# TensorE's column-half groups put next to each other, x and the ranks in other PSUM banks, and three moves on ScalarE and VectorE, in an attention + routed FFN kernel

## What is computed

```python
qkv = x @ W_attn + b_attn                       # [2, 2048, 768], 16 heads of 16
scores = einsum('bhtd,bhsd->bhts', q, k) / 4    # causal and j >= i - 64, per head
out = softmax(scores) @ v
x = layernorm(x + out @ W_proj + b_proj)
expert_idx = argmax(softmax(x @ Wr.T))          # one expert per token
inter = sum_e mask_e * gelu(x @ W1[e] + b1[e])
y = inter @ Wo + bo + x
out = layernorm(layernorm-with-gamma-beta(y) + x)
```

## Time and profile before

| what | us |
|---|---|
| median of 3 runs | 527.08 (524.29 to 529.04) |
| the profiled execution, its time | 529.32 |
| the profiled execution, its span in the trace | 527.6 |
| TensorE busy, share of the span | 486.1, 92% |
| VectorE busy | 427.4, 81% |
| ScalarE busy | 355.8, 67% |

### The profile page before, as it was taken

The page is one execution under the profiler, slowest core; times in us unless marked ns, Lnnn a source line. Parts: engine busy times, 40 slices in busy tenths (PEclk is TensorE's granted clock), DMA queues, the critical chain, the costliest instruction groups (busy, mean ns, idle before and its releaser), DMA issues. The chain is left out here.

```text
span 527.6 us, 24512 instructions
## 1 busy us (share of the span) xinstructions
PE 486.1 (92%) x8574; PEld 429.5 (81%) x8574; DVE 427.4 (81%) x1122; ACT 355.8 (67%) x796; POOL 321.6 (61%) x563
## 2 busy tenths in 40 slices
PE   7899999999999999899968797999999999999980
PEld 6778888888888888788857686888999999999970
DVE  5658888778977898778887567999999989999882
ACT  6576868677776877586857564666666766766850
POOL 8712545454464546354546447777888878888773
PEclk9999999999999999999999899999999999999996
DMA  7785768886778697686772122222345654532100
GB/s 200 194 240 174 205 206 235 209 206 186 231 207 220 183 253 193 193 229 191 187 197 58 42 63 62 73 62 64 83 117 187 199 175 162 171 130 79 44 23 8
DMA packets 90184, 80.96 MB, mean 153 GB/s; under 512 B 36502, under 2 KB 83871, under 8 KB 90018
## 3 DMA queue, kind: packets, MB, share of 16 engines
q1 hardware_dynamic: 86720, 70.95, 48.5%
q0 software_dynamic: 3248, 8.41, 4.7%
q10 hardware_dynamic: 98, 0.04, 0.0%
HBM read 43.50 MB, written 23.55 MB: 127 GB/s over the span
## 5 line engine op out<-in xcount | busy, mean ns | idle before, releaser
L1407 PE MATMUL ps<-v_even,w_hi 128*128 128x128 f16 x1024 | 141.2, 219 | 0.9 <-issue 0.8
L1389 PE MATMUL ps<-wo_hi,ks 128*128 128x256 f16 (+1 forms) x576 | 128.5, 273 | 7.3 <-DVE ks L1090 6.4
L833 ACT ACTIVATE probs<-ps,b1T 128x128 f32<-128x128 f32 (+1 forms) x312 | 85.5, 360 | 67.4 <-PE ps L1407 65.6
L1407 PE MATMUL ps<-v_even,w_lo 128*128 128x128 f16 x512 | 108.2, 219 | 0.1
L1407 PEld LDWEIGHTS ps<-v_even,w_hi 128*128 x1024 | 96.8, 98 | 3.9 <-issue 1.6
L1161 DVE TENSOR_REDUCE mx<-ps 128x4 bf16<-128x512 f32 x128 | 82.8, 684 | 10.2 <-PE ps L1458 9.7
L743 POOL CAST att_hi<-att 128x256 f16<-128x256 f32 x32 | 12.6, 394 | 114.7 <-DVE att L1218 114.7
L1389 PE MATMUL ps<-wo_lo,ks 128*128 128x256 f16 (+1 forms) x288 | 78.5, 273 | 0.0
L1090 DVE TENSOR_TENSOR ks<-probs,ks 128x512 f16<-128x512 f32 (+1 forms) x72 | 69.2, 961 | 9.0 <-ACT ks L840 5.5
L1507 PE MATMUL ps<-v_odd,probs 128*64 128x17 f32 x1024 | 69.7, 210 | 2.5 <-issue 2.5
L852 ACT ACTIVATE probs<-ps 128x512 f32<-128x512 f32 x128 | 69.5, 611 | 3.1 <-PE ps L1484 2.1
(11 more groups left out here) (246 smaller groups left out, 1279.2 us busy)
## 6 DMA issues: line engine op xcount, KB each, us to landing
qk_s<-qk_room SPq DMA_DIRECT2D x32, 256.0 KB, 3.0
w_in<-in_L_ffn_W_dram SPq DMA_DIRECT2D x16, 512.0 KB, 5.8
v_odd<-slots SPq DMA_DIRECT2D x64, 128.0 KB
qs<-qk_s SPq DMA_DIRECT2D x16, 384.0 KB
ks<-qk_s SPq DMA_DIRECT2D x16, 384.0 KB, 5.6
ks<-qk_s SPq DMA_DIRECT2D x32, 144.0 KB
v_even<-v_odd SPq DMA_DIRECT2D x63, 68.0 KB, 3.6
qk_s<-qk_room SPq DMA_DIRECT2D x32, 128.0 KB, 2.6
```

The costliest lines, as they stand in the source:

```text
L833: last = nc.scalar.activation(g[1 - p][:, ic, n * w:(n + 1) * w], ps_h[1 - p][:, half, col + n * w:col + (n + 1) * w], ACT.Gelu, bias=b1T[ ...
L1389: ins = mm(ps_y[p][0:m], h[p][hs][:, ic, 0:m], wo[ws][:, ic, :], start=n == 0, stop=n == 3 * IC - 1)
L1407: up_ins = mm(ps_h[1 - p][:, half, col + m * w:col + (m + 1) * w], weights(ws, m, k, ic), sT[1 - p][ss][:, k, at], start=k + n == 0, stop= ...
```

## The change

TensorE: in all iterations but 0, `scores(0)` and `scores(1)` move behind the projection and the transposes of x, so that the half groups follow each other. x's transposes write bank 4 and wait for `exps(0)` of the iteration before. The ranks write bank 6 (the last pair bank 1), no longer wait for `v_out` and `lx_done`, and `values(0)` waits for `place_done` in place of the projection. `mx` is 128 columns wide, so its transposes are full groups. ScalarE: v's copy goes between `maxima_rows(0)` and `maxima_rows(1)`. VectorE: `y` and `logits` go ahead of `maxima(0)`; the w1 split goes ahead of the copy `attT`. Both engines: two halves of w1 in each even iteration and none in an odd one, in place of one in each.

```diff
-        mx = [sb(f"mx{k}", [P, P - ALIGNED], bf16) for k in range(2)]
+        mx = [sb(f"mx{k}", [P, P], bf16) for k in range(2)]
...
         def ps_x(t):
-            return ps[:, 0 if t >= LEAD else 4 + t % 2, 0:CC * P].rearrange("p (k t) -> p k t", k=CC)
+            return ps[:, 4 if t >= LEAD else 4 + t % 2, 0:CC * P].rearrange("p (k t) -> p k t", k=CC)
...
-        ps_rank = ps[:, 1, 320:320 + 3 * E].rearrange("p (a e) -> p a e", a=3)
+        def ps_rank(pair):
+            return ps[:, 6 if pair < TILES // 2 - 1 else 1, 320:320 + 3 * E].rearrange("p (a e) -> p a e", a=3)
...
-        ps_mx = ps[0:P - ALIGNED, 2, 0:P].bitcast(bf16).rearrange("p (e m n) -> p e m n", e=2, m=CC)
+        ps_mx = ps[:, 2, 0:P].bitcast(bf16).rearrange("p (e m n) -> p e m n", e=2, m=CC)
...
         def w1_halves(it):
-            halves_at = range(it - 1, it) if it < TILES - 3 else range(2 * it - TILES + 2, 2 * it - TILES + 4)
+            halves_at = range(it - 2, it if it % 2 == 0 else it - 2) if it < TILES - 3 else range(2 * it - TILES + 2, 2 * it - TILES + 4)
...
# ScalarE
+                cur = a_tile(it)
+                if cur:
+                    act.wait_ge(mxT_done, it + 1)
+                    maxima_rows(0)
                 if a_tile(it + 1):
...
                         v_odd[m % VRING][:, :, 0:HD], ps_v[:, 0:C].rearrange("p (h d) -> p h d", d=HD), ACT.Copy)\
                         .then_inc(v_out, 1)
-                cur = a_tile(it)
                 if cur:
-                    act.wait_ge(mxT_done, it + 1)
-                    maxima_rows(0)
                     maxima_rows(1)
...
# VectorE
-                maxima(0)
-                maxima(1)
-                for t in turned(it) if it > FIRST else ():
-                    x_low(t)
                 if a_tile(old):
...
+                maxima(0)
+                maxima(1)
+                for t in turned(it) if it > FIRST else ():
+                    x_low(t)
...
+                for n in w1_halves(it):
+                    split_w1(n)
...
                     nc.vector.tensor_copy(attT[:, :, :, :], ps_attT).then_inc(attT_out, 1)
-                for n in w1_halves(it):
-                    split_w1(n)
...
# TensorE
                         wait(pe, att_done, done)
+                        wait(pe, place_done, (done - 1) // 2)
...
-                scores(0)
+                    scores(0)
+                    scores(1)
                 if a_tile(old):
...
-                    wait(pe, place_done, old // 2)
...
-                scores(1)
                 for t in turned(it):
...
                     if t >= LEAD:
-                        pe.wait_ge(qkh_done, t)
-                        pe.wait_ge(qkl_done, t)
+                        wait(pe, exp_done, 4 * (it - 1) + 1)
...
+                if it != 0:
+                    scores(0)
+                    scores(1)
                 values(0)
...
                     pe.wait_ge(onehot_done, old // 2 + 1)
-                    pe.wait_ge(v_out, upto(it + 1))
-                    pe.wait_ge(lx_done, upto(it + 1))
```

More of the change, by code:

```diff
@@ L858, in maxima_rows @@
                     nc.scalar.activation(q.rearrange("p (i h) n -> p i h n", i=STRIPS),
-                                         ps_mx.rearrange("p e m n -> p (e m) n").unsqueeze(1)
+                                         ps_mx[0:P - ALIGNED].rearrange("p e m n -> p (e m) n").unsqueeze(1)
                                          .broadcast_to([P - ALIGNED, STRIPS, 2 * CC, BLK]),
@@ L912, in _ @@
                         .then_inc(v_out, 1)
-                cur = a_tile(it)
                 if cur:
-                    act.wait_ge(mxT_done, it + 1)
-                    maxima_rows(0)
                     maxima_rows(1)
-                if cur:
                     exps(0)
@@ L1258, in _ @@
                     nc.vector.tensor_copy(attT[:, :, :, :], ps_attT).then_inc(attT_out, 1)
-                for n in w1_halves(it):
-                    split_w1(n)
                 if a_tile(old) and old % 2 == 1:
                     dve.wait_ge(rank_done, pair + 1)
-                    nc.vector.tensor_tensor(place[pair % 2][:, :, :], ps_rank,
+                    nc.vector.tensor_tensor(place[pair % 2][:, :, :], ps_rank(pair),
                                             place[1 - pair % 2][:, 2:3, :].broadcast_to([P, 3, E]), ALU.add)\
@@ L1651, in _ @@
                     pe.wait_ge(onehot_done, old // 2 + 1)
-                    pe.wait_ge(v_out, upto(it + 1))
-                    pe.wait_ge(lx_done, upto(it + 1))
-                    both = ps_rank[:, 0:2, :].rearrange("p a e -> p (a e)")
+                    rank = ps_rank(old // 2)
+                    both = rank[:, 0:2, :].rearrange("p a e -> p (a e)")
                     mm(both, before[:, :], onehot[:, 1:3, :].rearrange("p a e -> p (a e)"), start=True, stop=False)
                     mm(both, ones_b[:, :], onehot[:, 0:2, :].rearrange("p a e -> p (a e)"), start=False, stop=True)
-                    mm(ps_rank[:, 2, :], ones_b[:, :], onehot[:, 1, :], start=True, stop=False)
-                    mm(ps_rank[:, 2, :], ones_b[:, :], onehot[:, 2, :], start=False, stop=True).then_inc(rank_done, 1)
+                    mm(rank[:, 2, :], ones_b[:, :], onehot[:, 1, :], start=True, stop=False)
+                    mm(rank[:, 2, :], ones_b[:, :], onehot[:, 2, :], start=False, stop=True).then_inc(rank_done, 1)
                 scores_t(2)
```

## The result

The changed kernel takes 536.73 us (534.27 to 539.94, 4 runs) against 526.56 before: a ratio of 1.0178, 95% interval 1.0129 to 1.0227. The forecast was 516.5 in 510 to 523.5. It is slower, outside the range on its upper side. Medians here are over all executions of a kernel; ratios take, on both sides, only those within 1.5% of the kernel's fastest.

The account below looks back on a forecast made before the run. TensorE set the pace, with ScalarE's chain last after the change: 26 iterations x 0.44 = 11.4, ranks 0.6, first maxima 0.4, wo splits -1.9, last iterations 0.1, together 10.6 us off 527.08, giving 516.5, range 510 to 523.5.

Parts of the forecast that it names:

- The joints: TensorE's switches between half and full groups, eight per iteration, about 0.10 us each; removing them was to save 0.58 per iteration.
- x to scores(0): TensorE's joint after x's transposes, replacing x to values; forecast to change the cost by 0, bounds 0 and +0.10.
- The stall of values(0) on the exponentials: TensorE's values(0), ready at 4.55 us after the maxima's transposes, was to wait for exps(2) until 4.66.
- between them comes v's copy, 0.38 long and about 0.29 from start to start.: On ScalarE the copy between the maxima's rows overlaps its neighbours by 0.09 to 0.10, so rows(1) end at 2.52.
- The bound that I gave (0.41): Upper bound in us for v's copy from start to start on ScalarE, read from 171.54 to 171.95.
- Moving the copy is worth about nothing: On ScalarE, with v's copy ahead of the rows, rows(1) would end at the same 2.5 us after the maxima's transposes.
- It fits, 0.25 left before.: In even iterations VectorE's two w1 splits, 1.28 us, fit its 1.53 us of idle time ahead of attT; cost 0.
- I leave those as they are: Single TensorE stalls that no semaphore explains, 3.6 us in the values alone, and a first block's masks were taken as unchanged.
- the 11.4: The attention loop's main gain in us: 26 iterations x 0.44, from 8.18 to 7.74 each.
- I take 0.1: Iterations 28 to 31, with two joints fewer at most and TensorE waiting for POOL: between -0.5 and +1.0 us in all.
- Rival B: VectorE's y and logits delay maxima(0), scores(2) waits, the iteration stays at 8.18; 526 us, chance 0.17.
- C: Rival: scores(2) waits for the DMA of the keys' second half; 13 us slower, 540 us, chance 0.05.

Follow-up runs that it names:

- v_back: The changed kernel with v's copy put ahead of both rows of the maxima again; 533.44 us, ratio 1.0123 to the kernel before.
- v_split_back: The changed kernel with v's copy ahead of the maxima's rows and the w1 splits behind attT again; 529.37 us, ratio 0.9942 to the kernel before.
- joints_only: The kernel before with TensorE's part alone (moved scores, banks, mx of 128 columns), ScalarE's and VectorE's orders untouched; ratio 0.9998.
- v_between: The kernel before with v's copy between the two rows of the maxima alone; ratio 1.0128.
- split_ahead: The kernel before with the w1 halves alone: two in even iterations, the split ahead of attT; ratio 1.0071.
- mx_wide: The kernel before with mx of 128 columns alone; ratio 0.9986.

## Why the prediction was wrong

**Right.** The joints: half to full costs 0.10, and with them gone the chain through ScalarE makes the iteration 7.74 by the forecast, 7.75 in v_back and v_split_back, 7.79 in joints_only. x to scores(0) cost nothing more (0.31 with the joint). By the Trainium skill's drain at a mode change (TensorEngine Tiling (Array Packing), Key Properties) the same joints were to go, and did. The stall of values(0) on the exponentials was there, and the FFN stage didn't change beyond 0.7 us.

**Wrong, step by step.**

1. *"between them comes v's copy, 0.38 long and about 0.29 from start to start."* It measured 0.43, with nothing overlapped on either side, and took 0.1 of overlap from the rows too: 2.77 for rows(1), not 2.52. The bound that I gave (0.41) was from the row that I didn't take. v_back puts the price at 0.25 of an odd iteration (7.75 for 8.00), v_between at 0.26 (8.42 for 8.16). "Moving the copy is worth about nothing" was the mistake.
2. *"It fits, 0.25 left before."* It failed three ways. The splits don't take 1.28 there: beside POOL's work (that this is the reason was not tested) the first lasts 1.15, and both take 1.67, more than the 1.53 of idle time (split_ahead, where `lx` is on time). `lx` waits for v's copy, which the same change moved, so in the changed kernel they start 1.1 later. And attT had one more reader than I named: scores_t(3), which shares bank 7 with it (`wait(pe, attT_out, done + 1)`), stands in TensorE's order ahead of the projection. So the deadline was some 0.25 earlier. The splits ahead of attT alone cost 0.18 per even iteration; with the copy moved as well, TensorE waited 0.38 in 11 of the 13, and the shortest pair was 16.33 where 15.5 was forecast.
3. *"I leave those as they are"*, of the stalls without a releaser, and the clock of 1.00 taken as given. This was the largest up to iteration 27: joints_only has every joint gone and little of the waits of steps 1 and 2 (0.2 and 0.3 us), and gained nothing. Its stalls were 10 us against 3 to 5, and half clock came in a stretch that had none. The sum also took iteration 17, an odd one, for all 26: with the second kind of stall, as in both profiles of before, the even ones gain 0.1 at most, and 13 x 0.44 = 5.7 us of the 11.4 rested on them.
4. *Iterations 28 to 31, "I take 0.1".* From 27 to 31 it was +5.9 us, at a clock of 0.68 and 0.78: over half of the loss, and its cause stays open.

Rival B's kind (VectorE gets the gain) was nearest, but its place was attT and not maxima(0), and no rival held the clock. C, the one rival that was slower, is not in the changed kernel's profile: no wait for the keys stands among TensorE's. Its mechanism is real all the same: in v_split_back, with iterations of 7.75, TensorE waited 1.0 and 0.4 us for them in iteration 19. What stays open is why the stalls at the boundaries grow when the scores are moved, what the second kind is, and what exactly lets the clock fall.

No kernel here beats the one before by more than is uncertain; the nearest is v_split_back at 0.9942 (0.984 to 1.0043).

## What to carry to other kernels

Shortening TensorE by its joints pays only if the engine behind it has time: price the neighbour by widening one joint alone (mx_wide) or by adding a known delay (v_between) first. When several edits are made at once, follow every semaphore of every moved instruction to its next reader on each engine, bank sharing included, since idle time that one edit fills another edit may already have moved. A duration read in one place need not hold in another, either: the split that takes 0.68 behind attT took 1.15 ahead of it, beside POOL's work. And before believing the period of a quiet iteration, compare the granted clock of the stage, the sum of "issue" idle time, and odd with even iterations in more than one profile: here the shortest period fell by 0.4 and the time didn't.

## What the runs showed of the hardware

- Adjacent ScalarE instructions overlap by about 0.1 us (1.92 for two of 1.00), but not a row write of 32 partitions beside a copy of 128: starts are 1.03 and 0.41 apart.
- TensorE stalls of 0.2 to 2.3 us lie at numbers 194 and 195 modulo 256 of its stream, at some of these places and not at others, and fall on other matmuls when 64 instructions are put ahead.
- Stalls of 1 us and more in the half groups were often (22 of 27) followed by a stretch at 1.2 GHz (v_back: 0.57 over 4 us) in the kernels with the scores moved; before kept 2.4 GHz after one of 1.57.
- Widening a stationary operand from 32 to 128 columns halved its block, 0.22 to 0.11 us.
- A VectorE split of 128x512 that takes 0.68 us took 1.15 beside POOL's L745 and L751, and beside the two splits L751 and L752 took 0.64 and 0.65 in place of 0.19 (split_ahead).
